# A small layer turned round: weights stationary in a neighbour network, its result carried across by twelve transfers a tile

## The reference, cut to what matters

```python
topk_val, topk_idx = jax.lax.top_k(logits, K)            # K = 15 neighbours of each row
...
rel = jnp.concatenate([G, feat_a[..., None], delta[..., None]], axis=-1)   # 17 features
h = jax.nn.gelu(rel @ W1 + b1, approximate=False)         # 64 wide
h = jax.nn.gelu(h @ W2 + b2, approximate=False)           # 64 wide
z = jnp.tanh(h @ Wc + bc)                                 # Wc: 64 x 2
mix = jnp.where(keep, (h @ Wm + bm)[..., 0], -jnp.inf)    # Wm: 64 x 1
w = jnp.nan_to_num(jax.nn.softmax(mix, axis=-1))
gx, gy = (z[:, 0, :, :, 0], z[:, 0, :, :, 1])             # a point in a 16 x 16 palette
...                                                       # bilinear weights at (gx, gy)
V = jnp.einsum('btkd,btk->btd', samples, w[:, 0])
y = jnp.einsum('btd,dm->btm', V, Wo[0])
```

## Time and profile before

| | |
|---|---|
| median of 3 runs (lowest to highest) | 1595.28 us (1595.07 to 1597.09) |
| the profiled execution, its own time | 1594.69 us |
| its span, first to last instruction | 1592.5 us |
| busy: PE, PE's weight loads, DVE, ACT, POOL | 1301.1, 861.7, 1089.6, 842.2, 902.2 us |
| mean granted TensorE clock | 0.873 |

### The profile page before, as it was taken

The page is one execution under the profiler, slowest core; times in us unless marked ns, Lnnn a source line. Parts: engine busy times, 40 slices in busy tenths (PEclk is TensorE's granted clock), DMA queues, the critical chain, the costliest instruction groups (busy, mean ns, idle before and its releaser), DMA issues.

```text
span 1592.5 us, 47322 instructions
## 1 busy us (share of the span) xinstructions
PE 1301.1 (82%) x18392; PEld 861.7 (54%) x18501; DVE 1089.6 (68%) x4635; ACT 842.2 (53%) x2247; POOL 902.2 (57%) x1398
## 2 busy tenths in 40 slices
PE   3667678797889788887979798898978988788886
PEld 1333445454556555656556464656546565656654
DVE  2788677687778778787777777877866755464452
ACT  1233344464475555657564655475654646456665
POOL 2445666576658566666646565656645446455431
PEclk9686778897989889898989898898968888899999
DMA  5000000100000000000000000000000000000000
GB/s 159 2 1 10 27 18 18 29 9 23 6 25 9 25 7 17 17 11 24 17 22 8 18 14 14 20 7 24 9 18 14 7 27 10 26 15 21 5 3 7
DMA packets 27211, 29.57 MB, mean 19 GB/s; under 512 B 12097, under 2 KB 22114, under 8 KB 26978
## 3 DMA queue, kind: packets, MB, share of 16 engines
q0 software_dynamic: 8304, 16.73, 3.8%
q1 hardware_dynamic: 18674, 9.72, 2.2%
HBM read 25.11 MB, written 2.29 MB: 17 GB/s over the span
## 4 chain that ended last, share of the span: by engine, by line
PE 47%; DVE 22%; issue 10%; ACT 8%; POOL 8%; another core or an unknown queue 1%; SPq 1%; DMA 1%; DVEq 0%; POOLq 0%; ACTq 0%
DVE ps L963 4%; PE ps L665 3%; PE ps L523 3%; PE ps L717 3%; PE ps L747 3%; PE ps L563 3%; DVE ps L955 3%; PE ps L739 2%; PE ps L690 2%; PE ps L577 2%; PE ps L587 2%; PE ps L604 2%; PE ps L855 2%; ACT sb L1602 1%
## 5 line engine op out<-in xcount | busy, mean ns | idle before, releaser
L963 DVE TENSOR_TENSOR_SCAN ps<-ps,sb 128x47 f32<-128x47 f32 (+3 forms) x1024 | 271.3, 265 | 43.6 <-DVE ps L955 0.5
L1792 POOL DMA_INDIRECT sb<-table,sb x240 | 240.8, 1003 | 98.9 <-issue 55.3
L955 DVE TENSOR_TENSOR ps<-sb,ps 128x24 f32<-128x24 f32 (+3 forms) x1024 | 193.7, 189 | 15.4
L1656 POOL TENSOR_TENSOR sb<-sb 128x1 f32<-128x1 f32 x128 | 73.1, 571 | 221.4 <-DVE sb L898 220.7
L523 PE MATMUL ps<-sb 128*128 128x512 bf16 x496 | 162.0, 438 | 16.6 <-issue 10.2
L587 PEld LDWEIGHTS ps<-sb 32*32 32x32 f32 x2032 | 43.3, 110 | 123.9 <-issue 66.1
L577 PE MATMUL ps<-sb 32*32 32x32 f32 x2032 | 71.5, 213 | 41.5 <-DVE sb L935 34.6
L577 PEld LDWEIGHTS ps<-sb 32*32 32x32 f32 x2032 | 42.5, 111 | 113.2 <-DVE sb L935 58.5
L587 PE MATMUL ps<-sb 32*32 32x12 f32 x2032 | 65.5, 190 | 46.0 <-DVE sb L971 34.6
L1301 ACT ACTIVATE sb<-sb 128x128 f32<-128x128 f32 x128 | 62.9, 493 | 73.1 <-POOL sb L1658 72.8
L523 PEld LDWEIGHTS ps<-sb 128*128 128x128 bf16 x605 | 59.3, 109 | 62.5 <-issue 27.5
(11 more groups left out here) (310 smaller groups left out, 3739.4 us busy)
## 6 DMA issues: line engine op xcount, KB each, us to landing
sb<-table,sb POOLq DMA_INDIRECT x240
sb<-in_cs SPq DMA_DIRECT2D x16, 128.0 KB
table<-sb SPq DMA_DIRECT2D x17, 64.0 KB, 1.5
sb<-in_x SPq DMA_DIRECT2D x4, 256.0 KB, 7.8
sb<-dscr SPq DMA_DIRECT2D x64, 2.0 KB
out<-sb SPq DMA_DIRECT2D x16, 64.0 KB
sb<-in_mdn POOLq DMA_DIRECT2D x1, 512.0 KB, 9.9
sb<-in_wex SPq DMA_DIRECT2D x1, 512.0 KB, 7.4
```

The costliest lines, as they stand in the source:

```text
L955: e.tensor_tensor(at(psP, p + ROW - 3 - 2 * m, [ROW, 3], [2, m], [1, 2]), AC[:, row(n, k), :, HIST - 2 * m:HIST].rearrange("p r (a b) -> p ...
L963: e.tensor_tensor_scan(at(psD, 16 + k + COMB * skip, [COMB, 3 * ROW - skip]), at(psP, p + skip, [1, 3 * ROW - skip]), Q[:, i % 32, skip:3 ...
L1656: e.tensor_tensor(st[:, 11:12], st[:, 10:11], mhalf[:, 0:1], ALU.pow).then_inc(*s.G("lr"))
L1792: e.indirect_dma_start(GA[:, k, :], None, table[0:128 * i + 128, :] if i else table0, bass.IndirectOffsetOnAxis(u[:, k:k + 1], 0)).then_in ...
```

## The change

Three edits, and the orders written out anew.

1. The third layer takes `wcm` (now 64 rows x 3, the same for both halves) as the stationary side and lets all 512 columns of `H2[p]` stream past: one product for each (p, q), four in all, in one piece, into a bank of its own. The result has feature j on partition 64p+32q+j and (query, neighbour) along the row.
2. It must be turned to have the query on the partition. ACT copies the bank to `p_.zs` (a new piece, "zs"), SP issues twelve transfers from `p_.zs` to `p_.zr`, each from one partition to 32 partitions, 32 pieces of 64 bytes (a new piece, "ZD" below), and DVE's z piece waits for all twelve and reads `p_.zr`.
3. The outer products walk through the four parts (rows 0 or 64) x (columns 0, 32, 64, 96) in turn. Their number, eight pieces of eight, is the same.

The diff without the strings (`pb` and `bank` as before):

```diff
@@ -268,7 +268,7 @@
     wq = sb([128, 384])
     woT, bias, onesb = sb([128, 128]), sb([128, 520], BF16), sb([128, 128], BF16)
     wip, wo2, PT = sb([128, 256]), sb([128, 128]), sb([128, 129 * 16])
-    w1p, w2p, wcm, b12, bcm = sb([128, 256]), sb([128, 128]), sb([128, 6]), sb([128, 2]), sb([128, 3])
+    w1p, w2p, wcm, b12, bcm = sb([128, 256]), sb([128, 128]), sb([128, 3]), sb([128, 2]), sb([128, 3])
     wsi, wso, wex, wga = sb([128, 512]), sb([128, 128]), sb([128, 1024]), sb([128, 8])
     LG = sb([128, T])
     lqkv, lwo = sb([128, 384]), sb([128, 128])
@@ -417,7 +417,7 @@
     p_.G = ev("pal_G", LN_G + ["g1", "ga", "gb", "gc", "gd", "r", "n1", "n2"])
     m_ = Stage()
     m_.P = ev("mix_P", ["t0", "t1", "t2", "t3", "gm", "h0", "h1", "k0", "k1", "z", "op", "mm"])
-    m_.A = ev("mix_A", ["t0", "t1", "t2", "t3", "h0", "h1", "k0", "k1", "th", "ex", "ab", "rl", "c"])
+    m_.A = ev("mix_A", ["t0", "t1", "t2", "t3", "h0", "h1", "k0", "k1", "zs", "th", "ex", "ab", "rl", "c"])
     m_.X = ev("mix_X", ["x"])
     m_.V, m_.V0 = ev("mix_V", ["cl", "z", "mx", "xy", "rc", "nw", "wt"]), ev("mix_V0", ["z"])
     m_.G = ev("mix_G", ["ux", "uy", "u4"])
@@ -435,6 +435,7 @@
     hats, crd, crdT, WT = sb([128, 1536]), sb([128, 96]), sb([128, 96]), sb([128, 256])
     p_.bb, p_.r, p_.h, p_.n, p_.it = sb([128, 512]), one([128, 256]), one([128, 256]), two([128, 16]), one([128, 128])
     p_.u, p_.s, p_.csb, p_.z = two([128, 16], U32), two([128, 160]), one([128, 256]), sb([128, 48])
+    p_.zs, p_.zr, p_.zd = sb([128, 512]), sb([128, 48]), ev("pal_zd", ["z"] * 12, 16)
     p_.rl, p_.lb, p_.ub = sb([128, 512]), sb([128, 512]), sb([128, 1])
     p_.H1, p_.H2 = [[PT[:, x + 512 * p:x + 512 * p + 512] for p in range(2)] for x in (0, 1024)]
     table, table0, dscr = t["table"], t["table0"], t["dscr"]
@@ -728,24 +729,23 @@
                 b = bank(("pal", "k", p, c), m_.A.at(f"k{p}", c))
                 w.wait_ge(*m_.A.at(f"h{p}", c))
                 e.matmul(b[:, :], w2p[:, :], p_.H1[p], start=True, stop=True).then_inc(*m_.P(f"k{p}"))
-            hv = [p_.H2[p].rearrange("p (c k) -> p c k", k=16) for p in range(2)]
-            for k in range(15):
-                if k % 4 == 0:
-                    yield
-                    w.wait_ge(*m_.A.at("k1", c))
-                for p in range(2):
-                    for q in range(2):
-                        rows = slice(64 * p + 32 * q, 64 * p + 32 * q + 32)
-                        x = e.matmul(pb[rows, 3 * k:3 * k + 3], hv[p][:, :, k], wcm[:, 3 * q:3 * q + 3], start=True, stop=True)
+            yield
+            b = bank(("pal", "z", c), m_.A.at("zs", c))
+            w.wait_ge(*m_.A.at("k1", c))
+            for p in range(2):
+                for q in range(2):
+                    rows, to = slice(64 * q, 64 * q + 64), 64 * p + 32 * q
+                    x = e.matmul(b[to:to + 3, :], wcm[rows, :], p_.H2[p][rows, :], start=True, stop=True)
             x.then_inc(*m_.P("z"))
-            for k in range(32):
-                if k % 4 == 0:
+            for k in range(16):
+                if k % 2 == 0:
                     yield
                     w.wait_ge(*m_.G.at("u4", c))
-                for g in range(2):
-                    rows, to = slice(64 * g, 64 * g + 64), 64 * g + 32 * (k // 16)
-                    x = e.matmul(pb[to:to + 32, 16 * (k % 16):16 * (k % 16) + 16], hats[rows, 512 + 32 * k:544 + 32 * k],
-                                 hats[rows, 16 * k:16 * k + 16], start=True, stop=True)
+                for u in range(2):
+                    for g in range(2):
+                        rows, to, n = slice(64 * g, 64 * g + 64), 64 * g + 32 * u, 16 * u + k
+                        x = e.matmul(pb[to:to + 32, 16 * k:16 * k + 16], hats[rows, 512 + 32 * n:544 + 32 * n],
+                                     hats[rows, 16 * n:16 * n + 16], start=True, stop=True)
             x.then_inc(*m_.P("op"))
             for k in range(8):
                 if k % 2 == 0:
@@ -1146,10 +1146,10 @@
             e.scalar_tensor_tensor(out=p_.rl[:, :], in0=pb[:, :], scalar=p_.ub[:, :], in1=p_.lb[:, :], op0=ALU.min,
                                    op1=ALU.max).then_inc(*m_.V("cl"))
             z3 = p_.z[:, 0:45].rearrange("p (k j) -> p k j", j=3)
-            b3 = pb[:, 0:45].rearrange("p (k j) -> p k j", j=3)
+            b3 = p_.zr[:, :].rearrange("p (j k) -> p k j", j=3)[:, 0:15, :]
             yield
             w.wait_ge(*m_.A.at("ex", c - 1))
-            w.wait_ge(*m_.P.at("z", c))
+            w.wait_ge(*p_.zd.at("z", c))
             if i:
                 e.tensor_tensor(z3, b3, bcm[:, :].unsqueeze(1).to_broadcast([128, 15, 3]), ALU.add).then_inc(*m_.V("z"))
             else:
@@ -1507,6 +1507,10 @@
                 w.wait_ge(*m_.P.at(f"k{p}", c))
                 e.activation(p_.H2[p], bk.of["pal", "k", p, c][:, :], ACT.Gelu,
                              bias=b12[:, 1:2]).then_inc(*m_.A(f"k{p}"))
+            yield
+            w.wait_ge(*p_.zd.at("z", c - 1))
+            w.wait_ge(*m_.P.at("z", c))
+            e.activation(p_.zs[:, :], bk.of["pal", "z", c][:, :], ACT.Copy).then_inc(*m_.A("zs"))
             z3 = p_.z[:, 0:45].rearrange("p (k j) -> p k j", j=3)
             yield
             w.wait_ge(*PV.at("zb", 0))
@@ -1961,6 +1965,13 @@
                 at = 128 * i + 64 * (q // 2)
                 e.dma_start(p_.lb[32 * q + 16:32 * q + 17, :].rearrange("a (c k) -> a c k", k=16),
                             dscr[at:at + 64, :].rearrange("(c u) k -> u c k", u=2)[q % 2:q % 2 + 1]).then_inc(*p_.rel("rel"))
+            yield
+            w.wait_ge(*m_.A.at("zs", c))
+            w.wait_ge(*m_.V.at("z", c - 1))
+            for g in range(4):
+                for j in range(3):
+                    e.dma_start(p_.zr[32 * g:32 * g + 32, 16 * j:16 * j + 16],
+                                p_.zs[32 * g + j:32 * g + j + 1, :].rearrange("a (c k) -> a c k", k=16)).then_inc(*p_.zd("z"))
 
         def ffn8(c):
             i = c % NT
@@ -2029,11 +2040,9 @@
     for q in range(4):
         w1p[32 * q:32 * q + 17, 64 * q:64 * q + 64] = b("W1")
     w2p = np.zeros((128, 128), np.float32)
-    wcm = np.zeros((128, 6), np.float32)
     for q in range(2):
         w2p[64 * q:64 * q + 64, 64 * q:64 * q + 64] = b("W2")
-        wcm[64 * q:64 * q + 64, 3 * q:3 * q + 2] = b("Wc")
-        wcm[64 * q:64 * q + 64, 3 * q + 2:3 * q + 3] = b("Wm")
+    wcm = np.tile(np.concatenate([b("Wc"), b("Wm")], axis=1), (2, 1))
     mup, mdn = np.zeros((128, HU), np.float32), np.zeros((128, 2, 2, 4, 128), np.float32)
     for x in range(8):
         g, j = x // 4, x % 4
```

All five strings of `ORDER` and `FILL` are new. The digits of the new `FILL` add up to 681. SP's string, which has the new transfers in it:

```diff
-        "pppppmpppmppmppppmpppmpmpppppmppmpeeeppempepppmppmpppmepppmpppmppmepepepeemeeeee",
+        "ppppmpmpmppmppmpppmpmmppmpmpeemppmppmpmpmppmpmepepmppempmeppmepmppmpmpepmpmpepmpmpepepmmpmmeeeee",
```

More of the change, by code:

```diff
@@ new lines @@
+        "osgssososossosgsssssoosssaspsaassssfaaasaaspaspfsgsmpssmpsmsmsgommpsspfsoosmmmsmmmosossgmsmsmsomssosfmssafpa"
+        "ssassssapaassaasasgmmsmssmgpmmsmmpspmsmmsosmssooososfssmmsmmsgmosopsmpmsmmsamagasmsmmmgsmpmsasaasmasaaffssbs"
+        "bbsspmmsmpmbmmbpbpsmmbsbbsmsmmmslolsgsososooslsllsflsmlmgsmmplmlmsmlsmosposmccmcsccsamcmsgccamscsamfsssmsdma"
+        "pdsddsdmagafdspdaaasddssgssbssbbsmospmgfmmoopmmsbpbbosobbbmmmsmslmlmsgmsmmslslolslsollspmgmsmpplsmalmmmaasmg"
+        "cccsccmcsmsmpcscmscsmsfeeseeeasemdessspaesdaeddsdsfagaammdmmmdsddbmsbmmsobsmsmpmsmpooosobbbfmmsbbsmbsmlopslo"
@@ new lines @@
+        "bpbsmbsbmmmmmposmsmlmosplpmsmsllsasllllsmsmaalsmlppcsccccscccceeesemmdemsememmmamedaseasddasdmmmaamsdddsdbsb"
+        "bmmompsmpoombobbobbbpmmmmmmlmlpmmpllolllolppmmallaamcccccccccaeadeeaedmddedemmsmaaaeeddmmmdebdmbbmmmmpmpmbbb"
+        "mmbbpbmmmppbpblblmmmmmpmlmlllllbmbbmbmblbllclccccclllclcllcelldeedeedmedemdmmmmmmeemmmmcmmcmcddddbmbbcmcmmmm"
+        "cmmmbcbbmcbbbmcmlmldmedeedddellllelelmmmmmmmedmdeddlelmmmmcccbccbbccccbbbebeeebbededelldddelllllleldldddcccc"
+        "cccccedeededdedeeeddeddeeeeeeeee",
@@ new lines @@
+    "POOL":
+        "ffffggfggggfffggggfggggffgfggggofooooogooogfagfpfpppppggggogogfooogoooohahghhhhhhhhhhphfhhffppppgopgoooggooo"
+        "oofhahmhmhgfhghhhhfmhphhhhfhgoopppgpooooooogpgfaghhghghhhhhhhmhbmhpgmhfhggphpflppofollllolololoooogfpcagghgh"
+        "dhghghhhhhhddhdhdhmfmgbmgfpofhghogogogoloopploollppllllapggfchghghhehhdhhmhmhhghmddddbphfhoogfhpfpooopoogolo"
+        "ppgllflallllchhhghhhghhmgmhehdhmfhbphfhddddpoohggfpplooooolloollplllggapcghghfhgehdhhmhghmhhdhdmdbdfhfhpfgoh"
+        "ghoppopooooolpofgpllllalglghlcghghmhghgmhhhmhfhedhhbphghfhddfddooooopfoloppoopllglpllalglgghchhghhmhmhhedfhm"
+        "ggbhphhhddddoppohhpooooplofogpolglalllfllgchhghghhhmmehdmgghfhbhhphdgdpddphoohphoooplooogopllfllalfllgfgghch"
+        "ghghhmhmhehdhmhhbghfphddhdhdpoopppgooolooofollllfllaplfcghgghghheghdhfhghmmhghhhhdmdddhghbopogooooooofplpppf"
+        "fplllgllgllgacmmggeggmdhhhhhhhhhdhhdhddbhoohphooooppoppogolpalllgllllcmmhhehdmhhhhhhhhhddddbhphhooppppoolopo"
```

(4 more changed lines are left out.)

186 lines of the change are left out of this document (82 added, 104 removed).

## The result

The changed kernel takes 1654.16 us (median of 4 runs, 1639.77 to 1658.76) where the kernel before, on the same chip, takes 1596.18 (1595.07 to 1597.95): a ratio of 1.0347, interval 1.0279 to 1.0415. By the medians it is 58 us slower, by the ratio 55; the forecast was +74, 1669 us. A ratio here is taken over all fast runs and need not be the quotient of the medians; where the two part, both are given. The profiled execution took 1658.76 us, with a span of 1656.6 and a granted clock of 0.860.

A forecast was written before the change was run, and what follows sets the result against it. The bound was taken as five closely coupled lists in fixed order, PE the fullest, not one engine. A loss of 16 x 6.4 = 102 us less 28 gave +74 on 1594.7: 1669 us, range 1586 to 1715.

The forecast's parts named there:

- The road: New path from PE to DVE's z: ACT copy 0.75, twelve issues 6.9, landing 1.6; 9.2 us, bounds 6.3 and 10.
- The stall at z: DVE stands at z for 7.4 us a tile: 9.2 less 1.0 of lateness and 0.8 given by the list.
- What of it reaches the end: Of DVE's wait at z, 6.4 us a tile, bounds 0 and 9, lengthens the execution: 102 us over 16 tiles.
- compounded rival: Delay at z grows through SP's held-up list and POOL's list with its gathers, 2.5 us a tile: 1710, chance 0.12.
- PE's gain: Both edits on PE save 1.8 us x 16 = 29 us of its time, 28 off the end, bounds 5 and 55.
- The third layer's eight records: Four new products on PE, two row parts abreast: 2.0 us a tile, bounds 2.0 and 4.0, saving 1.3.
- The outer products: On PE, four parts bring records from 0.0167 to 0.0116 us each, saving 0.5 us a tile, bounds 0 and 1.2.
- the stops stay, as their number stays: PE's stops for instructions at the outer products remain, since the number of instructions is unchanged; no saving counted.
- Cheap transfers: Rival: the twelve transfers at z are hidden or overlap, path to DVE 3 us: 1586 us, chance 0.16.
- Issues like L1951's: Rival: SP's issues at L1951's 0.325 us, path to DVE 6.3, 3.5 us a tile lost: 1623, chance 0.17.
- a stall half absorbed: Rival: half of DVE's wait at z is absorbed; same time as the 1623 us rival, within its chance of 0.17.
- Row parts in series: Rival: third layer's row parts run one after another on PE, 32 us more: 1700 us, chance 0.07.

## Why the prediction was right, and where its sizes were off

**The road: right.** Forecast 0.75 for the copy, 6.9 for the issues, 1.6 for the landing, 9.2 together. In tile 6 the copy with its hand-over took 0.7 us, the twelve issues 7.1 from the first start to the last (0.65 apart, one small gap among them), the landing 1.72: 9.6 from the end of L738 to z. Taking L1962's 0.60 us and not L1951's 0.325 was the choice that decided, and the median of 192 issues is 0.590. The run with three transfers shows that it isn't the number of pieces that makes them dear.

**The stall at z: right.** 7.4 us a tile forecast, 113.7/16 = 7.1 measured; and it is no gap of the lists, since it goes with the number of transfers (26.6 and 235.6 us for 3 and 24 on one chip, 113.7 for 12 on the other), and from 3 to 24 the time follows it.

**What of it reaches the end: the mechanism right, the size too large.** Forecast 102 us. The version in which DVE turns has the same products and no road. By the medians it gains 37.6 us, and the changed kernel loses 58.0 in the first comparison and 51.0 in the second: together 89 to 96 us. By the ratios it gains 24 and the changed kernel loses 55 and 59: 79 to 83 us. So the road and the new lists together cost 79 to 96 us, 4.9 to 6.0 a tile, where I had 6.4 for the road alone. The lists have to be taken off that, for which I had put 0, fills and all; on the other chip they cost 8 us with the old third layer and 6 with the turn on DVE (0.55% and 0.44%, both near the noise), and on this one nobody measured them. That POOL and ACT wait behind z is the same delay, as I had put it: POOL's 129.5 us behind L1164 don't come on top, since from 3 to 24 transfers the time grows by DVE's wait alone; and the compounded rival (1710) fell. On the chip of 1488 us the whole of the added wait reached the end.

**PE's gain: the mis-sized terms.** Forecast 29 us of PE's own time and 28 off the end. PE's own came to 45 + 25 = 70 us, in two terms:

- The third layer's eight records. I took two row parts abreast, 2.0 us. Measured in tile 6 and again in tile 15:

```profile
1545.89 1.04 PE L738 MATMUL ps<-sb 64*3 64x512 f32 x8
```

1.04 us for eight records of 512 columns, where four in the earlier trace rows take 1.98. All four products run abreast (eight records in the time of two), also the two that read the same 64 rows of the array and differ only in their columns. My bounds (2.0 and 4.0) did not hold it: I had priced row parts, and forgotten that the four products stand on four column parts as well. The Trainium skill (TensorEngine Tiling (Array Packing), Restrictions and Gotchas) says that different row tiles cannot use one PSUM bank at once. The four write one bank, each to partitions of its own, so after L759 the trace contradicts it a second time, for products that share no partition of the bank.
- The outer products. Within a piece 16 records take 0.32 us at a granted clock of 1.00 (2.4 GHz), so (0.32 - 0.18)/15 = 0.009 each, not 0.0116. And "the stops stay, as their number stays" was wrong in size for the changed kernel: 13.0 us of issue in place of 21.2.

Of these 70 us, the end got 24 to 38, by the version that turns on DVE (its own PE time fell by 69 us, and DVE has 11.2 us more). That is a third to a half. I had written "on the chain half of the time and more" and then, since the list was packed anew, taken 28 of the 29 us. So two errors worked against each other in this term, a saving of less than half its size and a share of two to three times its size; that 28 came near to 24 to 38 is luck.

**The sum.** 102 - 28 = +74 forecast; +51 to +59 measured. Since the road's figure above is the loss plus the gain, it can't check the sum by itself. With the gain of the medians both terms are off by about 10 us in the same direction; with that of the ratios nearly all of the error is in the road. The runs don't decide between the two. The scan's end moved by 70 us ("60 us or more"), and what follows it gained 6.

**The rivals.** Cheap transfers (1586): refuted by the 0.59 us. Issues like L1951's (1623): refuted likewise; a stall half absorbed, which gives the same time, doesn't fit 4.9 to 6.0 us of 7.1 a tile either. Row parts in series (1700): refuted by 1.04. On the cheap transfers one thing has to be put right: I said that the rows contradict 0.05 us of dispatch. That section of the Trainium skill (DMA: Bandwidth & Descriptors, Anatomy of one DMA) is on transfers that GpSimd issues, and all of these are SP's. Their 0.59 us shows that the figure doesn't carry over to them, and no more. What I had not listed at all is that PE's side of the sum belongs to the chip: where L739 has no stops, both edits on PE bring 0.3%, and next to nothing is set against the road. The changed kernel itself wasn't run there. Between 3 and 24 issues the time grows by 10.0 us for each issue of a tile, so twelve would give about 1508 + 90 = 1598 us, 7% over the kernel before; an estimate.

Open: what makes the same program stop on one chip and not on the other. The rows show where the stops lie and that they come with a lower granted clock, not their cause; and with two chips, each used at another time, the chip itself is only the likeliest difference. The two groups account for 54 of the 121 us between the spans; the rest wasn't followed up. Open too is what the changed kernel takes on the chip without them, and how the 70 us that PE saves divide between the path, the clock and nothing.

## What to carry to other kernels

Price a transfer that replaces a direct read by its issues in series, from the row of the nearest shape, and multiply by the tiles before asking what it saves: here 12 x 0.6 us stood on the chain against a layer of 4 us a tile. A small result that has to be turned can be turned by the engine that reads it, here DVE in blocks of 32 x 32: 0.7 us in place of 9.6. And a gain that consists of instructions saved should be measured on more than one chip before it is believed.

## What the runs showed of the hardware

- The same program, the kernel before, takes 1488 us on one chip and 1597 on another. With the outer products alone changed, the 1920 records of L739 have 18.6 us of issue ahead of them on the latter, in stops of some 0.5 us, and none (0.0) on the former, with granted clocks of 0.869 and 0.912. The 4096 Gram records L717 have 7.7 us on both.
- Four products of 64 rows x 3 columns, two on each half of the rows, each with 512 columns of other data, run abreast into one bank, each on partitions of its own: eight records in 1.04 us, where four full ones take 1.98.
- SP needs 0.58 to 0.59 us for each issue within SBUF, for 32 pieces of 64 bytes and for 128 alike; for 128 pieces from SBUF to DRAM (L1951) it needs 0.32.
- DVE transposes 128x512 f32 from a PSUM bank in 0.70 us, in blocks of 32 x 32, with the columns read at a stride of 16.
- A z that comes later by transfers issued in series lengthened this kernel by as much: 209.0 us more of waiting, 210.6 us more of time, at granted clocks of 0.902 and 0.852.
